# TensorE's scatter halves in groups that take turns with the experts' outputs, the scores and the turned lists

## What is computed

```python
xn = (x - mu) * rsqrt(var + eps) * gamma + beta          # per feature, over all 4096 tokens
q = (xn @ w_q.T) ...                                     # 2 halves x 8 heads x 128
sim = einsum('pbnhd,hkpd->pbnhk', q, keys)               # 2 x 8 x 32 scores a token
s, i = top_k(sim, 8)                                     # the best 8 of 32, each half and head
scores, pk = top_k(s[0][..., :, None] + s[1][..., None, :], 8)   # the best 8 of 64 sums
idx = ...                                                # 8 heads x 8 experts of 1024, each token
o = gelu(einsum('bnd,bnhkd->bnhk', x, key_in[idx])) * softmax(scores)
y = einsum('bnhk,bnhkd->bnd', o, key_out[idx])
out = layernorm(x + y)
```

## Time and profile before

| | |
|---|---|
| time, median of 3 runs | 503.56 us (501.24 to 507.07) |
| the profiled execution's own time | 506.19 us |
| its span in the profile | 504.1 us |
| TensorE, busy share of the span | 73% in 10,097 matmuls |
| VectorE, busy share | 86% |
| ScalarE, GpSimd, busy share | 48%, 46% |
| mean granted clock of TensorE | 0.786 of full |

### The profile page before, as it was taken

How to read it: one execution, slowest core, us unless ns; L and a number is a source line. 1 busy time by engine, 2 the same in 40 slices (tenths; PEclk the granted TensorE clock), 3 DMA queues, 4 the chain that set the end, 5 groups by cost and what they waited for, 6 DMA issues and landing times.

```text
span 504.1 us, 24229 instructions
## 1 busy us (share of the span) xinstructions
PE 366.8 (73%) x10097; PEld 268.3 (53%) x10097; DVE 431.7 (86%) x2755; ACT 243.5 (48%) x398; POOL 232.1 (46%) x311
## 2 busy tenths in 40 slices
PE   5979855166647778786888689768787678878755
PEld 3445543034443557465748474646477347746655
DVE  1557986999999689989999999899999997995923
ACT  2897564355324433574365337443754472445222
POOL 1023350542449344646556474647382925282610
PEclk9979956678656877889797678877987796579769
DMA  8900000000000000000000000000000000000001
GB/s 241 180 1 1 1 1 0 1 1 5 3 5 2 3 4 3 5 3 25 6 1 4 25 5 1 6 25 3 3 6 25 3 3 4 25 3 4 23 5 44
DMA packets 7661, 8.95 MB, mean 18 GB/s; under 512 B 896, under 2 KB 6912, under 8 KB 7424
## 3 DMA queue, kind: packets, MB, share of 16 engines
q1 hardware_dynamic: 6976, 7.34, 5.5%
q10 hardware_dynamic: 576, 0.07, 0.1%
HBM read 5.31 MB, written 2.10 MB: 15 GB/s over the span
## 4 chain that ended last, share of the span: by engine, by line
PE 47%; DVE 17%; issue 14%; POOL 5%; ACT 4%; ACTq 0%; DVEq 0%; POOLq 0%
PE psum L895 17%; PE psum L871 13%; PE psum L882 9%; PE psum L851 6%; DVE idx L623 3%; DVE vals L615 3%; DVE picked L648 2%; DVE arena L679 2%; POOL code L259 2%; POOL arena L286 2%; DVE arena L683 1%; DVE arena L682 1%; DVE arena L676 1%; ACT L434 1%; POOL ixf L254 1%
## 5 line engine op out<-in xcount | busy, mean ns | idle before, releaser
L871 PE MATMUL psum<-arena 64*64 64x16 f16 x8192 | 94.0, 180 | 77.5 <-issue 67.1
L871 PEld LDWEIGHTS psum<-arena 64*64 64x64 f16 x8192 | 86.2, 117 | 94.5 <-issue 85.5
L895 PE MATMUL psum<-ko,arena 64*128 64x128 f32 x1024 | 90.2, 353 | 2.0 <-issue 2.0
L895 PEld LDWEIGHTS psum<-ko,arena 64*128 64x128 f32 x1024 | 86.7, 264 | 2.9 <-issue 2.5
L623 DVE FIND_INDEX8 idx<-vals,sims 128x8 uint32<-128x32 f32 x512 | 82.7, 186 | 0.0
L286 POOL TENSOR_TENSOR arena<-arena 128x512 f32<-128x512 f32 x60 | 77.7, 1328 | 4.3 <-ACT arena L426 4.3
L882 PE MATMUL psum<-x1T,trn 128*64 128x256 f32 x512 | 68.3, 423 | 12.6 <-ACT arena L434 12.6
L679 DVE TENSOR_TENSOR arena<-iota,listsT 128x4096 f16<-128x4096 f16 x32 | 74.9, 2339 | 0.0
L426 ACT ACTIVATE arena<-psum 128x1024 f32<-128x1024 f32 x32 | 32.6, 1018 | 72.5 <-PE psum L871 72.5
L882 PEld LDWEIGHTS psum<-x1T,trn 128*64 128x64 f32 x512 | 36.6, 152 | 51.1 <-ACT arena L434 24.3
L239 POOL TENSOR_TENSOR cand<-vals 128x128 f32<-128x128 f32 x16 | 9.4, 588 | 118.0 <-DVE vals L615 118.0
(11 more groups left out here) (117 smaller groups left out, 563.7 us busy)
## 6 DMA issues: line engine op xcount, KB each, us to landing
x<-in_L_attn_x_dram SPq DMA_DIRECT2D x8, 256.0 KB, 4.8
out_dram<-nat SPq DMA_DIRECT2D x7, 256.0 KB, 2.1
ko<-in_L_ffn_key_out_dram SPq DMA_DIRECT2D x2, 512.0 KB, 9.7
nat<-in_L_ffn_key_in_dram SPq DMA_DIRECT2D x2, 256.0 KB, 9.7
nat<-in_L_ffn_keys_dram SPq DMA_DIRECT2D x2, 128.0 KB, 5.6
out_dram<-nat SPq DMA_DIRECT2D x2, 128.0 KB, 1.7
nat<-in_L_attn_W_delta_dram SPq DMA_DIRECT2D x1, 64.0 KB, 2.8
nat<-in_L_attn_W_in_dram SPq DMA_DIRECT2D x1, 64.0 KB, 2.8
```

Source lines behind the costliest of these rows:

```text
L871: end = pe.matmul(psum[64 * e:64 * e + 64, at:at + NJ], hotx[rows, g, :, e], hotw[rows, part, g, :, e], start=(part == 0), stop=(part == 1))
L895: end = pe.matmul(y2[:, e, m % 2] if m < NS - 1 else y_last[:, e], gl[rows, m % 4, j, :], ko[rows, j, :], start=(j == 0), stop=(j == NJ - 1))
```

## The change

Only TensorE's program changes, and in it only the order. `scores` takes the groups of tokens that it is to do. `scatter` and `experts_out` can be called for a part of their steps, and wait for the two semaphores that all steps share only in the first part. A new function, `scatter_and_out`, puts four steps of a scatter half (32 matmuls) and two values of j of `experts_out` (4 matmuls) by turns, six times; then two groups of scatter follow each other, and the last four values of j. It is used for the newer half in passes 3 to 16, and for the very last half with `experts_out(14)`. In the older half, the score matmul of group 0 now stands behind 12 steps, the lists behind 22 and the score matmul of group 1 behind the lists.

```diff
@@ -844,9 +844,9 @@
                 end.then_inc(s["x1T_mm"], 1)
             pe.wait_ge(s["x1T_evac"], NCH)
 
-            def scores(m):
+            def scores(m, tokens=(0, 1)):
                 wait(pe, "xn_done", m + 1)
-                for t in range(2):
+                for t in tokens:
                     wait(pe, "sims_ready", m * 2 - 1 + t)
                     pe.matmul(b_sim[t], xn[:, t], msim[:, :], start=True, stop=True).then_inc(s["sim_mm"], 1)
 
@@ -859,8 +859,9 @@
                 end.then_inc(s["lists_mm"], 1)
 
             def scatter(m, hf, first=0, last=32):
-                wait(pe, "p_evac", m * 2 + hf)
-                wait(pe, "hot_done", m * 2 + (hf + 1))
+                if first == 0:
+                    wait(pe, "p_evac", m * 2 + hf)
+                    wait(pe, "hot_done", m * 2 + (hf + 1))
                 for k in range(first, last):
                     g = 32 * hf + k
                     for e in range(2):
@@ -883,18 +884,27 @@
                                             trn[:, 9 + r, 64 * b:64 * b + 64], tokens[:, e], start=True, stop=True)
                     end.then_inc(s["g_mm"], 1)
 
-            def experts_out(m):
-                wait(pe, "zf_done", m // 2)
-                for j in range(NJ):
+            def experts_out(m, first=0, last=NJ):
+                if first == 0:
+                    wait(pe, "zf_done", m // 2)
+                for j in range(first, last):
                     if m < NS - 1:
                         wait(pe, "a_done", m * 4 + j // 4 + 1)
                     else:
                         pe.wait_ge(s["a_tail"], 2)
                     for e in range(2):
                         rows = slice(64 * e, 64 * e + 64)
-                        end = pe.matmul(y2[:, e, m % 2] if m < NS - 1 else y_last[:, e], gl[rows, m % 4, j, :], ko[rows, j, :], start=(j == 0),
-                                        stop=(j == NJ - 1))
-                end.then_inc(s["y2_mm"], 1)
+                        end = pe.matmul(y2[:, e, m % 2] if m < NS - 1 else y_last[:, e], gl[rows, m % 4, j, :],
+                                        ko[rows, j, :], start=(j == 0), stop=(j == NJ - 1))
+                if last == NJ:
+                    end.then_inc(s["y2_mm"], 1)
+
+            def scatter_and_out(m, hf, done):
+                for r in range(8):
+                    scatter(m, hf, 4 * r, 4 * r + 4)
+                    if r < 6:
+                        experts_out(done, 2 * r, 2 * r + 2)
+                experts_out(done, 12, NJ)
 
             scores(0)
             for m in range(NS + 1):
@@ -902,24 +912,24 @@
                     lists_turned(NS - 1)
                 if m >= 2:
                     scatter(m - 2, 1, 0, 12)
+                if m + 1 < NS:
+                    scores(m + 1, (0,))
+                if m >= 2:
+                    scatter(m - 2, 1, 12, 22)
                 if 1 <= m < NS:
                     lists_turned(m - 1)
+                if m + 1 < NS:
+                    scores(m + 1, (1,))
                 if m >= 2:
-                    scatter(m - 2, 1, 12, 32)
-                if m + 1 < NS:
-                    scores(m + 1)
+                    scatter(m - 2, 1, 22, 32)
                 if m % 2 and m < NS:
                     experts_in(m // 2)
-                if m == NS:
-                    wait(pe, "lists_evac", NS)
-                    experts_out(NS - 3)
-                if m >= 1:
+                if 3 <= m:
+                    wait(pe, "lists_evac", m)
+                    scatter_and_out(m - 1, 0, m - 3)
+                elif m >= 1:
                     scatter(m - 1, 0)
-                if 3 <= m < NS:
-                    wait(pe, "lists_evac", m)
-                    experts_out(m - 3)
-            scatter(NS - 1, 1)
-            experts_out(NS - 2)
+            scatter_and_out(NS - 1, 1, NS - 2)
             experts_out(NS - 1)
```

## The result

The changed kernel takes 524.95 us (median of 4 runs, 521.69 to 531.93) against 505.16 us before, measured again beside it: a ratio of 1.038, 95% interval 1.033 to 1.044. Forecast were 498.0 us and a range up to 509. Ratios and their intervals are of executions that the chip ran in its faster state, so they can differ a little from the quotient of two medians. The profiled execution has a span of 521.9 us; before it was 504.1.

A forecast was written before the change was run, and what follows sets the result against it. VectorE was taken as the bound to about 457 us. The even sub-steps (-0.5 us) and the tail with the earlier start (-5.1) sum to -5.6; against the median of 503.56 us, 498.0 was predicted, range 489 to 509.

The forecast's parts named there:

- VectorE sets the pace: Whole kernel to about 457 us: VectorE is the bound, busy 431.7 of 504.1 us; TensorE matters only where VectorE waits.
- A gap is the wait for a block of 256 instructions: TensorE's scatter halves: gaps are waits for the next 128 pairs, 3.5 us a block (2.8 to 3.75).
- The lists come 1.7 us later in the even sub-steps: Older half: one score matmul and 80 scatter pairs ahead delay the lists, 11.1 us after the start becoming 12.8.
- forecast 1.2: Start of the even sub-steps' half: 1.2 us earlier (bounds 0.2 and 1.9), none in the first such half.
- L676's waits were to be 0.5 to 1.5 us in the even sub-steps: Sign of being right: VectorE's one-hot waits 0.5 to 1.5 us for lists there; over 2 us in each means wrong.
- In the odd sub-steps the lists have some 4 us of room and nothing happens: Older half of sub-steps with `experts_in`: some 4 us of room for the lists, so no effect was counted.
- A round's cost: Mixed newer half: scatter and output pairs priced by block, about 103 scatter in 0.95 us, 25 outputs in 2.1 us.
- The tail: From the half at 456.92 us to the end: 3.9 us shorter (1.9 at 3.75 us a block), 5.1 with the earlier start.
- the pace of the blocks: Mixed halves: a block's work takes 3.1 us, under the 3.5 us a block, gaining about 1.8 us a half.
- 1.0 us on ScalarE: End of the tail: after the last scatter pair at 31.2 us, 1.0 on ScalarE and 1.2 on VectorE.
- the lists come late: Rival, chance 0.12: the mix runs at half clock, 10.3 us a half, lists 2.6 us later still six times; 514 us.
- the gaps are not the fetch's: Rival, chance 0.05: gaps stay whole, interleaving gains nothing, lists stand 1.63 + 0.74 us further back; 515 us.

The follow-up runs named there:

- e7: The kernel before plus 21 unused float32 matmuls (42 pairs) ahead of the first scores; nothing else moved. Its single execution took 511.77 us.
- e6: The changed kernel plus six unused float32 matmuls ahead of the mixed half in the odd sub-steps, where TensorE idled: 516.35 us, ratio 1.030 to the kernel before.
- e3: The changed kernel with each mixed half in two rounds (16 steps, 8 values of j) instead of small groups: 507.36 us, ratio 1.007 to the kernel before.
- e5: The changed kernel with ScalarE's copy of the last sub-step's first scatter half moved ahead of the square root: 524.85 us, ratio 1.035 to the kernel before.
- e1: The changed kernel with its older half put back as before; newer halves and last half stay mixed: 507.64 us, ratio 1.010 to the kernel before.
- e10: The kernel before with newer halves mixed in two rounds, tail outputs in pieces around scatter halves, and ScalarE's copy ahead of its square root: 495.35 us, ratio 0.987.

## Why the prediction was wrong

**VectorE sets the pace: right.** Its busy time did not move (431.7 and 432.5 us), and the loss before the tail came in as waits of it (5.9 us more, of 6.3).

**A gap is the wait for a block of 256 instructions: right**, by `e7`. With the mix the gaps behind it shrank from up to 2.8 us to 1.5 and less before the tail, nearly as forecast (none over 1 us within a mixed half). In an even half at full clock the gain was there too: 320 pairs in 7.9 us, where the earlier trace rows has some 10.2 (361.38 to 371.6).

**The lists come 1.7 us later in the even sub-steps: about right, the waits not.** At 365.31 the lists came 12.4 us after the half began, forecast 12.8 with a like place in the block. Over the six even halves the distance is 0.4 to 1.4 us longer than before. Counted from VectorE's one-hots ahead of it (the second L676, at 355.04 before and 359.84 after), this half began 0.9 us earlier, forecast 1.2. But L676's waits were to be 0.5 to 1.5 us in the even sub-steps, and three of the five are 2.4 to 2.9. At 415.13 the lists were to come 12.4 us after the start and took 13.9, part of it at the half clock.

**"In the odd sub-steps the lists have some 4 us of room and nothing happens": this is the step that failed.** I had priced a mixed half once, for the even sub-steps, at some 9 us, and taken the odd ones for covered. The room itself was read too large: from the lists to L676 less the 1.05 us that the copy takes, the six odd sub-steps before had 1.5 to 4.3 us. The odd half can't begin before VectorE's hots, so whatever TensorE had gained ahead of it turned into idling (3.94 us at 383.79), and idling into the half clock. The half took 13.1 us and the lists came 17.7 us after its start (334.23 to 351.94), 12.3 before (333.26 to 345.57). That is 5.4 us more, where the room had been 2.5: five waits of 0.3 to 0.9 us in the odd sub-steps, `experts_in` late behind them, and the next even half too. With the odd halves at the full clock (`e6`) the last even half began at 453.8 us in the profile, 9.4 earlier, and ahead of the 456.9 of the kernel before, which is the gain that was forecast for this part and more. I had the half clock as a rival, at 10.3 us for a half and in the even sub-steps; it was in the odd ones, and 13.1 us because each of the 13 changes cost 0.16 us, 2.1 in all, and because the outputs cost 116 ns and not 101, 1.0 us.

**A round's cost.** The sum took the outputs at 85 ns and the scatter at 9.2 from unbroken runs, and no cost for changing from one to the other. A change is 0.11 us at full clock, 0.16 at half, and the 85 ns lie between the 62 at full and the 116 at half clock of `e3`. The two rounds of `e3` avoid ten of the changes and gave 17.6 us by medians, 3.1% by ratios, clock included.

**The tail: the larger part of the miss.** Counted from the start of its first half, -3.9 us were forecast and +11.5 came in the profile: 15.4 of the 23.4 us between forecast (-5.6) and profile (+17.8). It is the same step: the mixed halves were priced at the pace of the blocks, the clock left out, and the waits ahead of them at nothing. Three terms are missing. Both mixed halves ran at the half clock, 13.2 us each where I had reckoned some 9 (8.4 us in all). ScalarE's copy of the older half of sub-step 14 was covered by the outputs before the change; mixed, nothing stands between the two halves, and 1.16 us is open. (Between the last two halves the kernel before had such a wait too, 1.14 us at 483.40.) And the copy of the last but one half has no term at all: the sum's "1.0 us on ScalarE" is that of the last one. I had not looked at what stands ahead of it in ScalarE's row: a square root that waits for those outputs which the change moved to the end of the same half, 3.42 us (`e5`). They make 13.0 us of the 15.4. The last 64 output pairs took 5.8 us for the 4.5 reckoned; the 1.1 us left I can't name.

**The chances.** The rival "the lists come late", 514 us for 0.12, had the right two ingredients. (The nearest number, 515, was that of "the gaps are not the fetch's", whose mechanism `e7` refutes.) The condition of the late lists was held to be unlikely because the slow halves before stood behind long gaps that were to shrink. But in these traces the clock was down behind waits for hots as it had been behind gaps, and I did not ask where the time gained would be spent.

## What to carry to other kernels

Time that is won on an engine that is not the bound is spent in a wait, and for TensorE a wait can cost the clock of what stands behind it: follow the gain to the place where it is idled away before counting it. Mix two kinds of matmuls in few large pieces, as in `e3`, where the clock came back in five of six halves and most of the changes are saved, and only where TensorE arrives at work. And when a producer's steps are interleaved with another's, look up what the consumers' engines have written between the two: work that was ordered for the old sequence becomes a wait in the new one.

## What the runs showed of the hardware

**The granted clock of a finely mixed half went with what stood ahead of it.** In the changed kernel the halves directly behind `experts_in` ran at 1.00 (7.9 us). All but one of those behind waits of 1.2 to 3.9 us ran at 0.50 to their end (13.1 us), with TensorE's rows unbroken, and 0.50 was still granted in the older half and the scores that followed (396.9 to 403.9); within `experts_in` it was up again, and stayed up over a wait of 2.27 us (1.00 from 409.69 on). So a wait of a given length is not enough to tell what the clock does. Some halves behind waits of 1.2 to 2.1 us began at 1.00 and fell within three rounds (285.67 in the changed kernel, 282.01 in `e6`). In `e1` halves directly behind score matmuls at 0.50 rose within their first round. In `e3` the clock rose within five of six odd halves (mean 0.63 at 377.7). Six unneeded matmuls ahead of the half kept it up in three places of `e6` and raised it in three. Which property of the stream it is that raises the clock is not shown.

**Half the clock doesn't double everything.** Output pairs in runs of 32 went from 62 to 116 ns (1.9 times), scatter pairs in pieces of 128 from 9.2 to 14.1 ns (1.5 times).

**Changing between 64 x 64 float16 tiles and 64-row float32 tiles takes 0.11 us at full and 0.16 us at half clock**, an average worked out from groups of 32 and 8 against pieces of 128 and 32. The tile, the type and the PSUM target change together, and no run takes them apart.

**TensorE's instruction blocks can be counted.** Moving 42 pairs moved seven gaps by 42 or, around the block, 86 pairs. A stream of short matmuls at 9.2 ns a pair uses a block up in 1.2 us. From the start of a block to the start of the next it then took 2.8 to 3.75 us in the earlier trace rows and 4.0 in `e10` (474.28 to 478.30). In `e7` it was only 1.5 us at one place: a burst of 143 pairs at 318.80, the last 128 of them a block, with the next at 320.47. The Trainium skill, Runtime: NRT & Kernel Launch, section Instruction fetch mechanics, gives TensorE room for 2048 instructions, speaks of room for only two blocks a few lines on, and calls the fetch hidden; here the bursts of short pairs at the start of the even newer halves, in `e7`'s profile as before, all waited after at most 230 of them, 460 instructions, and the measurement decides: it is not hidden, and it fits the two blocks better than the 2048. How large the room is stays open.
